# A decoder kernel's routing: logits and residual from the output projection, one scan for the places, one-hots on three engines

## Chip, core and metric

The kernel runs as one program on one core of a Trainium2 chip. The metric is the device time of one execution in microseconds (us). All operands are float32 unless said otherwise; the program is written by hand, with its own semaphores on each engine: PE (TensorE), DVE (VectorE), ACT (ScalarE), POOL (GpSimd) and SP (SyncE, which issues transfers).

## What is computed

Two decoder blocks on x of shape 32 x 64 x 128 (2048 tokens of 128 features), each sublayer followed by `x = layernorm(x + f(x))`. Block 0: a windowed self attention with its MLP, a causal windowed cross attention on a context, and a mixture of experts. Block 1: a linear attention, a recurrence, and a small attention on the seven best rows of each sequence. The change is about the end of the cross attention and the routing of the experts:

```python
# cross attention, last lines; then the norm
out = attn_out @ Wo.T + bo
x = _layernorm(x + out)
# experts: E = 8, K = 2, cap = 512
logits = xt @ wg
scores = softmax(logits)
gates_k, idx_k = top_k(scores, K)
gates_k = gates_k / sum(gates_k)
m = one_hot(idx_k, E) in the order (choice, token)
loc = sum((cumsum(m, axis=0) - 1) * m, axis=-1)
valid = loc < cap
disp = disp.at[idx_k, clip(loc)].add(xt * valid)
h = relu(disp @ w1 + b1); out = h @ w2 + b2
y = sum over the K choices of gates_k * valid * out[idx_k, loc]
```

## The kernel before, in words

The 2048 tokens are 16 tiles of 128 rows, worked in four quads of four tiles. Each engine runs its list in order; what another engine must wait for is a semaphore. A `Chain` object (`link`) makes an engine wait for its own last result.

**Self attention and its MLP.** `att_pe`, `att_dve`, `att_act` and `att_spread` (POOL, L383) work tile by tile. `norm1` on DVE and POOL norms the tiles behind it: POOL adds, takes the reciprocal root of the variance (`rstd_of`, L566 and L567), and makes three adds or products of a quad for the later residual (L682, L683, L685); DVE forms the shift (L1459) and then two columns of a bias (L1472). PE then loops over quads (L850 on): hidden layer (`hidden_self`, L814), the transposes of the next quad (L589), the keys and values of the cross attention (`keys_values`, L834 and L846), and the MLP's output (L863, bank 4). It works the keys of a quad only after DVE has taken the values before (`values_out`, L1513). DVE takes the MLP's output with L1488, norms it (`sum_quad`, L1491), adds the residual (`second_norm`, L1499) and norms again (`third_norm`).

**Cross attention.** The same helpers, with `add_bo` on POOL: after tiles 8 to 11 it forms `x_side = x + bo` for a quad (L709). DVE's step for a tile holds, among others, L493 (maximum), L509 and L511 (two steps on 16 elements) and L520. In the last two turns PE transposes the attention's output (`turn_out`, L925), ACT copies it (L1304), and PE multiplies by Wo (`project_out`, L931, one bank per quad). DVE adds `x_side` (L1536) and takes the statistics (L1479, L1482), POOL the root; DVE forms the shift of quads 0 and 1 and ACT norms them (L1310), DVE norms quads 2 and 3 (L544). SP stores each quad to `token_rows` (L634).

**Routing.** PE transposes the normed tiles (`ln_pe`, L589), ACT copies them (L595), PE multiplies by wg (`logits`, L915). DVE copies the logits (L1565), chooses twice (L1569 to L1576, eleven steps up to the second one-hot), and forms the gates around an exp of ACT (L1322). PE multiplies the one-hots by a matrix of ones and by one of earlier rows (L961, L962); DVE copies, scans (L1589) and combines these to the place of each choice (L1588 to L1613). It then builds two bf16 one-hots in four chunks, by slot (L1618) and by row (L1620), which PE multiplies in 32 products (L967); from that DVE computes which token row each place of an expert takes (L1628 to L1634, `place`). POOL gathers these rows with indirect transfers (`fetch`, L716) for four experts ahead, and scatters results (L730). Meanwhile ACT waits for DVE's L1638 with an Ln (L1329), forms `decay` and copies `wcomb` (L1333, L1335), after which PE runs ten filling matmuls (`keep`, L576) and the experts (`turn_in` L981, `hidden` L988, `output` L995).

## Time and profile before

| | |
|---|---|
| median of 3 runs | 444.09 us (440.9 to 446.13) |
| the profiled execution's own time | 440.14 us |
| its span in the profile | 438.3 us |
| PE busy | 365.4 us, 83% |
| DVE, ACT, POOL busy | 257.0, 194.5, 188.2 us |

The trace gives each instruction a start and a length in us from the span's start. An engine's idle time is shown with the one whose semaphore ended it. The chain of waits is followed back from the last instruction to whatever released each step. The granted clock is that of PE: 1.00 is 2.4 GHz, 0.50 is 1.2 GHz.

### The profile page before, as it was taken

To read this page: it belongs to the slowest core of one execution; us is meant where nothing else is said; L and a number is where in the kernel's file an instruction comes from. 1 tells how busy PE (TensorE), PEld (TensorE's weight loads), DVE (VectorE), ACT (ScalarE), POOL (GpSimd) and SP (SyncE) were. 2 spreads that over 40 slices of the span, in tenths; PEclk is the share of its full clock that TensorE was granted. 3 is DMA by queue.
4 is the path that set the end of the run, shared out by engine and by line. 5 is a ranking of instruction groups with operands and counts; after the bars stand their busy time and mean duration, and the time that the engine had idled before them with its cause. 6 is when DMAs were issued, how large, how long until landed. Compare 5 with 4: busy or idle time off the path is not lost.

```text
span 438.3 us, 8261 instructions
## 1 busy us (share of the span) xinstructions
PE 365.4 (83%) x3249; PEld 260.5 (59%) x3249; DVE 257.0 (59%) x742; ACT 194.5 (44%) x333; POOL 188.2 (43%) x232
## 2 busy tenths in 40 slices
PE   6999988999989999881489978797857988888780
PEld 2677775677767777761238756752635656765550
DVE  0788992689999899759600100022785788437430
ACT  1567775734577777521244433022362432124420
POOL 2234546853343520310376777772333437440002
PEclk9999999999999999995599999899889887859996
DMA  7999600000000000030011111117000000010000
GB/s 275 408 406 396 209 4 1 2 1 1 1 1 2 1 2 1 10 89 0 18 55 42 55 50 52 50 54 198 9 0 1 0 2 0 25 72 1 1 1 12
DMA packets 18358, 27.54 MB, mean 63 GB/s; under 512 B 2416, under 2 KB 13680, under 8 KB 17680
## 3 DMA queue, kind: packets, MB, share of 16 engines
q1 hardware_dynamic: 16208, 22.69, 14.5%
q0 software_dynamic: 2112, 4.33, 3.4%
q8 instruction: 26, 0.43, 0.4%
q14 instruction: 12, 0.10, 0.1%
HBM read 20.59 MB, written 6.42 MB: 62 GB/s over the span
## 4 chain that ended last, share of the span: by engine, by line
PE 57%; POOL 11%; DVE 11%; ACT 9%; issue 6%; DMA 4%; POOLq 0%; SPq 0%; DVEq 0%; ACTq 0%
PE bank L410 7%; PE bank L433 7%; PE bank L420 7%; PE bank L576 6%; POOL choice_rows L730 4%; POOL q_diag L716 4%; PE bank L589 3%; PE bank L995 3%; PE bank L863 3%; PE bank L988 2%; PE bank L814 2%; PE bank L393 2%; ACT x_tok L1310 2%; DMA q_diag<-in_q_self 1%; PE bank L872 1%
## 5 line engine op out<-in xcount | busy, mean ns | idle before, releaser
L576 PE MATMUL bank<-mask_bf,ident_bf 128*128 128x512 bf16 x206 | 59.5, 425 | 4.5 <-DVE mask_bf L1442 3.4
L493 DVE TENSOR_REDUCE neg_max<-bank 128x16 f32<-128x1024 f32 x34 | 41.5, 1222 | 19.4 <-PE bank L410 19.3
L383 POOL TENSOR_TENSOR scratch<-k_comp,con 128x512 f32<-128x512 f32 x32 | 33.4, 1047 | 37.6 <-PE bank L410 33.8
L465 ACT COPY probsT<-bank 128x1024 f32<-128x1024 f32 x34 | 34.4, 1012 | 26.3 <-PE bank L420 26.2
L716 POOL DMA_INDIRECT q_diag<-token_rows,place x32 | 30.8, 963 | 35.4 <-DVE place L1634 26.0
L476 ACT ACTIVATE probs<-probs 128x1024 f32<-128x1024 f32 x34 | 35.9, 1056 | 19.6 <-DVE probs L520 19.6
L433 PEld LDWEIGHTS bank<-v_pair,probsT 128*64 128x64 f32 x1088 | 34.7, 138 | 16.4 <-issue 10.8
L433 PE MATMUL bank<-v_pair,probsT 128*64 128x18 f32 x1088 | 37.9, 212 | 5.5 <-ACT probsT L465 4.6
L1665 DVE TENSOR_TENSOR probsT<-bank,mb 128x512 f32<-128x512 f32 x7 | 4.8, 691 | 62.2 <-PE bank L995 62.2
L410 PE MATMUL bank<-scratch,q_diag 64*128 64x256 f32 x272 | 39.5, 410 | 0.7 <-DVE scratch L383 0.5
L566 POOL TENSOR_SCALAR var_e<-mv 128x4 f32<-128x4 f32 x28 | 6.9, 247 | 75.8 <-DVE mv L1686 41.0
L420 PE MATMUL bank<-con,probs 128*128 128x128 f32 x272 | 36.9, 279 | 1.1 <-ACT probs L476 1.0
L576 PEld LDWEIGHTS bank<-mask_bf,ident_bf 128*128 128x128 bf16 x206 | 21.1, 109 | 27.2 <-issue 7.9
L730 POOL DMA_INDIRECT choice_rows<-probsT,place x32 | 31.2, 975 | 11.6 <-issue 8.8
L995 PEld LDWEIGHTS bank<-mw,hT 128*128 128x128 f32 x256 | 31.1, 197 | 4.5 <-issue 4.5
L995 PE MATMUL bank<-mw,hT 128*128 128x128 f32 x256 | 31.6, 280 | 0.9 <-ACT hT L1348 0.9
L410 PEld LDWEIGHTS bank<-scratch,q_diag 64*128 64x128 f32 x272 | 24.1, 190 | 13.9 <-issue 11.0
L420 PEld LDWEIGHTS bank<-con,probs 128*128 128x128 f32 x272 | 29.4, 141 | 3.2 <-ACT probs L476 1.8
L567 POOL TENSOR_TENSOR rstd<-var_e,neg_half 128x4 f32<-128x4 f32 x28 | 29.7, 1062 | 2.3
L988 PE MATMUL bank<-probs,mw 128*128 128x512 f32 x64 | 29.2, 599 | 1.5 <-ACT probs L1341 1.5
L1348 ACT ACTIVATE hT<-bank,mb 128x512 f32<-128x512 f32 x32 | 22.0, 687 | 18.2 <-PE bank L988 17.5
L589 PE MATMUL bank<-con,x_tok 128*128 128x128 f32 x80 | 19.1, 328 | 11.2 <-ACT x_tok L1310 7.1
(281 smaller groups left out, 678.8 us busy)
## 6 DMA issues: line engine op xcount, KB each, us to landing
mw<-in_mw SPq DMA_DIRECT2D x2, 2048.0 KB, 14.0
v_pair<-in_v_self SPq DMA_DIRECT2D x4, 576.0 KB, 11.2
q_diag<-in_q_self SPq DMA_DIRECT2D x4, 512.0 KB, 10.4
choice_rows<-hT SPq DMA_DIRECT2D x1, 2048.0 KB, 13.3
con<-in_const SPq DMA_DIRECT2D x1, 1249.5 KB, 15.1
k_comp<-in_k_self SPq DMA_DIRECT2D x4, 256.0 KB, 9.3
x_tok<-in_x SPq DMA_DIRECT2D x1, 1024.0 KB, 10.8
ctxT<-in_ctxT SPq DMA_DIRECT2D x1, 1024.0 KB, 9.6
```

The source lines that it names most:

```text
L383: mult(k_heads[:, i % 2], k_comp[:, i, :, None, :].to_broadcast([P, 2, HG, S]), hm, ALU.mult).then_inc(s["spread"], 1)
L410: last = nc.tensor.matmul(bank[:, 2 * (i % 2) + rg, g * 256:(g + 1) * 256], q_diag[r, i, g], k_heads[r, i % 2, g].rearrange("p h k -> p (h ...
L420: last = nc.tensor.transpose(bank[:, 4 + hp // 4, (hp % 4) * P:(hp % 4 + 1) * P], probs[:, i % 2, hp * P:(hp + 1) * P], ident)
L433: last = nc.tensor.matmul(bank[b * S:(b + 1) * S, 6 + i % 2, hp * VW:(hp + 1) * VW], probsT[:, i % 2, at:at + S], v_pair[:, 2 * i + b, hp] ...
L465: nc.scalar.copy(probsT[:, i % 2], bank[:, 4:6, :].rearrange("p a n -> p (a n)")).then_inc(s["evacuated"], 1)
L476: nc.scalar.activation(probs[:, i % 2], probs[:, i % 2], ACT.Exp).then_inc(s["exp"], 1)
L493: have_m = link.mark(nc.vector.tensor_reduce(m, sc, AX, ALU.max, negate=True))
L576: nc.tensor.matmul(bank[:, bk, :], ident_bf[:, :], mask_bf[:, 0, None, :].to_broadcast([P, 8, S]), start=True, stop=True)
L716: nc.gpsimd.indirect_dma_start(out=expert_x(e)[:, j], out_offset=None, in_=token_rows[:, :], in_offset=bass.IndirectOffsetOnAxis(ap=place[ ...
L730: nc.gpsimd.indirect_dma_start(out=choice_rows[:, :], out_offset=bass.IndirectOffsetOnAxis(ap=place[:, 1, at:at + 1], axis=0), in_=expert_ ...
L988: mm(bank[:, f], mw1[:, e, f * P:(f + 1) * P], probs[:, e % 2, 0:512], start=True, stop=True).then_inc(s_mh, 1)
L995: last = mm(cols4(out_bank(j), j), hT[:, v % 2, f, j * P:(j + 1) * P], mw2[:, v, f], start=f == 0, stop=f == FC - 1)
```

## The change

**Folding.** Products with wg are made ahead. Behind the self attention PE forms the column mean of wg and transposes Wo and bo; DVE makes `with_x = [ident | wg - mean]` and copies the transposes; PE, after the first `keys_values`, waits for these copies, forms Wo wg and bo wg, waits for DVE's copies of these, and goes on with L863. `with_o = [Wo | Wo wg]`.

**Projection.** For each tile PE adds the residual's product `xT x with_x` and `attention x with_o` in one PSUM group of 136 columns; the last eight are the logits before the norm's scaling. DVE adds a bias to these (`logits`), and bo to the first 128. The transposes, copies and products for the logits go, and POOL's `add_bo` too. For quad 3 ACT copies the projection, POOL adds bo and DVE takes the statistics after the choices. ACT norms all four quads, and the gates' difference is multiplied by rstd.

**Places.** The one-hots are bf16 (`chosen_bf`). Two products add up to the steps between one tile's place and the next, and DVE scans them straight from PSUM. Row and tile come from a division by rounding.

**One-hots.** The row one-hots are shared: chunks 0 and 1 on DVE, chunk 2 on ACT (eight Square and a Relu), chunk 3 as a subtraction on POOL and a comparison with zero on DVE. `token_rows` gets a zero row in front, so that a gather's place takes three steps. `place` comes first, and the gates after it. PE's filling matmuls change from 12 ahead of the choices to 16, and 16 more follow the rank products.

The diff's core:

```diff
             att_pe(pe, att["self"], NT, ident_bf[:, :], mb(0), True,
...
+            mm(bank[:, 4, 0:E], con_at("ones"), wg[:, :], start=True, stop=True)
+            tr(bank[:, 4, P:2 * P], wo[:, :], ident)
+            tr(bank[:, 4, 2 * P:3 * P], rows[:, 6], ident).then_inc(s_r["fold"], 1)
             pe.wait_ge(att["self"]["taken"], NT)
...
                 keys_values(q)
+                if q == 0:
+                    pe.wait_ge(s_r["folded"], 1)
+                    mm(bank[:, 4, 3 * P:3 * P + E], wo_turned, with_x[:, P:], start=True, stop=True)
+                    mm(bank[:, 4, 3 * P + E:3 * P + 2 * E], bo_turned, with_x[:, P:], start=True, stop=True).then_inc(s_r["fold"], 1)
                 if q == NQ - 1:
                     ln_pe(pe, ln["ln3"], 1, x_tok)
                 pe.wait_ge(s_hT, FC * q + FC)
                 if q >= 1:
                     pe.wait_ge(ln["ln2"]["stats"], 4 * q)
+                else:
+                    pe.wait_ge(s_r["folded"], 2)
...
             def project_out(q):
                 pe.wait_ge(s_oTs, q + 1)
                 for j in range(4):
-                    last = mm(cols4(2 + q, j), masked(q)[:, j * P:(j + 1) * P], wo[:, :], start=True, stop=True)
+                    if j % 2:
+                        residual(q, j)
+                    last = mm(projection(q)[:, j // 2, j % 2], masked(q)[:, j * P:(j + 1) * P], with_o, start=False, stop=True)
                 last.then_inc(s_wo, 1)
+
+            def residual(q, j):
+                t = 4 * q + j
+                mm(projection(q)[:, j // 2, j % 2], xT[:, t * P:(t + 1) * P], with_x, start=True, stop=False)
...
-            keep(2, 12)
+
+            keep(6, 16)
             pe.wait_ge(s_r["chosen"], 1)
-            oh = route("onehot", 2 * NT * E)
-            mm(bank[:, 1, E:256], con_at("ones"), oh[:, 0:256 - E], start=True, stop=True).then_inc(s_r["ranks"], 1)
-            mm(bank[:, 0, 0:256], con_at("earlier_row"), oh, start=True, stop=True).then_inc(s_r["ranks"], 1)
+            steps = bank[:, 0, 0:256].rearrange("p (e n) -> p e n", e=E)
+            oh = chosen_bf[:, :, :].rearrange("p n e -> p e n")
+            mm(steps, earlier_bf, oh, start=True, stop=False)
+            mm(steps[:, :, 1:], later_bf, oh[:, :, 0:TOPK * NT - 1], start=False, stop=True).then_inc(s_r["ranks"], 1)
+            keep(2, 16)
...
             norm_act("ln4", 1)
-            for q in range(NQ):
-                ln_act(act, ln["ln4"], q)
+            act.wait_ge(s_r["logits"], NQ)
+            cp(tiles22(work[:, NT - 4:NT]), projection(NQ - 1)[:, :, :, 0:P]).then_inc(s_oTs, 1)
+            norm_act("ln4", 2)
+
+            act.wait_ge(s_r["rows"], 1)
+            for n in range(16, 24):
+                off = link.mark(A(rank_hot[:, n], row_index_bf[:, :], ACT.Square, bias=route("row_of", TOPK * NT)[:, n:n + 1], scale=-1.0))
+            link.wait(off)
+            A(rank_hot[:, 16:24], rank_hot[:, 16:24], ACT.Relu, bias=con_at("ones")[:, 0:1], scale=-1.0).then_inc(s_r["exp"], 1)
+
+            norm_act("ln4", 3)
...
                 ts(cols[:, at:at + 2], cols[:, 0:2], con_at("own_half")[:, b:b + 1], HD ** -0.5, ALU.mult, ALU.mult)

+            dve.wait_ge(s_r["fold"], 1)
+            stt(with_x[:, P:], bank[:, 4, 0:E], -1.0 / P, wg[:, :], ALU.mult, ALU.add)
+            cp(wo_turned, bank[:, 4, P:2 * P])
+            cp(bo_turned, bank[:, 4, 2 * P:3 * P]).then_inc(s_r["folded"], 1)
+            cp(with_x[:, 0:P], ident)
+            cp(with_o[:, 0:P], wo[:, :])
...
                 values_out(q)
+                if q == 0:
+                    dve.wait_ge(s_r["fold"], 2)
+                    cp(with_o[:, P:], bank[:, 4, 3 * P:3 * P + E])
+                    cp(logit_bias, bank[:, 4, 3 * P + E:3 * P + 2 * E]).then_inc(s_r["folded"], 1)
...
+            cp(row_index_bf[:, :], con_at("row_index"))
+            cp(earlier_bf, con_at("earlier_row"))
+            ts(later_bf, con_at("earlier_row"), -1.0, 1.0, ALU.mult, ALU.add)
...
+            shift(ln["ln4"], 2)
+            dve.wait_ge(s_wo, NQ)
+            logits(NQ - 1).then_inc(s_r["logits"], 1)
+            dve.wait_ge(s_r["logits"], NQ)
...
+            dve.wait_ge(s_side, NQ + 1)
+            told_quad(ln["ln4"], NQ - 1, [link.n] * 4)
...
+            link(nc.vector.tensor_tensor_scan(run, con_at("scan_carry"), bank[:, 0, 0:256], 0.0, ALU.mult, ALU.add))
+            v_at = at.rearrange("p (n e) -> p n e", e=E)
+            link(tt(v_at, run.rearrange("p (e n) -> p n e", e=E), chosen_bf[:, :, :], ALU.mult))
+            link(nc.vector.tensor_reduce(rank, v_at, AX, ALU.add))
+            link(ts(tile_of, rank, 0.5 - P / 2, 1.0 / P, ALU.add, ALU.mult))
+            link(ts(tile_of, tile_of, ROUND, ROUND, ALU.add, ALU.subtract))
+            stt(row_of, tile_of, float(-P), rank, ALU.mult, ALU.add).then_inc(s_r["rows"], 1)
...
+            pool.wait_ge(s_r["rows"], 1)
+            tt(rank_hot[:, 24:32], row_index_bf[:, None, :].to_broadcast([P, 8, P]),
+               route("row_of", TOPK * NT)[:, 24:32, None].to_broadcast([P, 8, P]), ALU.subtract).then_inc(s_r["rows"], 1)
```

DVE's list after `rows` is then: `held`, the two parts of `told_bf`, the shift of quad 3, the four chunks, three steps to `place[:, 0]` (which release the gathers), two to `place[:, 1]`, the gates' difference times rstd, and after ACT's exp the gates and their validity.

## Rows read from the trace of the kernel before

**Rows 1.** The page's part 4: shares of the chain that ended last, by engine.
```profile
PE 57%; POOL 11%; DVE 11%; ACT 9%; issue 6%; DMA 4%; POOLq 0%; SPq 0%; DVEq 0%; ACTq 0%
```

**Rows 2.** Chain of waits, 70 to 96 us: start, us, what.
```profile
75.85 3.77 PE bank L863 x32
79.62 3.45 PE bank L814 x8
...
94.35 1.07 PE bank L834 x16
```

**Rows 3.** Timeline, 74 to 98 us: start, us, engine, line, operation [idle before <-releaser].
```profile
80.28 1.23 DVE L1459 SCALAR_TENSOR_TENSOR var_e<-mv,rstd 128x4 f32<-128x4 f32 x1 [3.95 <-POOL rstd L567]
...
82.77 1.38 DVE L1513 TENSOR_TENSOR v_pair<-bank,rows 64x512 f32<-64x512 f32 x2
82.79 1.27 POOL L685 TENSOR_TENSOR x_tok<-x_tok,rows 128x512 f32<-128x512 f32 x1
...
84.19 0.89 DVE L1488 TENSOR_TENSOR work<-bank,routing 128x128 f32<-128x128 f32 x4
```

**Rows 4.** Busy time in stretches: us, PE, PEld, DVE, ACT, POOL, granted PE clock, DMA.
```profile
199.00:199.50 0.50, 0.00 (x0) 0.00 (x0) 0.47 (x2) 0.14 (x1) 0.00 (x0) 0.58 0.00 0
...
219.50:220.00 0.50, 0.50 (x4) 0.25 (x3) 0.00 (x0) 0.00 (x0) 0.50 (x1) 0.94 0.45 123
```

**Rows 5.** Timeline, 134 to 159 us, beside the bias add.
```profile
151.57 1.28 POOL L709 TENSOR_TENSOR x_side<-x_tok,rows 128x512 f32<-128x512 f32 x1
...
151.79 1.08 DVE L509 TENSOR_SCALAR neg_max<-neg_max 128x16 f32<-128x16 f32 x1
...
154.61 1.11 PE L433 MATMUL bank<-v_pair,probsT 128*64 128x18 f32 x32 [0.80 <-DVE work L524]
```

**Rows 6.** Timeline, 174 to 222 us, the projection and norm.
```profile
176.62 1.06 PE L931 MATMUL bank<-wo,scratch 128*128 128x128 f32 x8
...
183.31 3.19 ACT L1310 ACTIVATE x_tok<-work,var_e,rstd 128x128 f32<-128x128 f32 x8
...
184.67 1.04 POOL L567 TENSOR_TENSOR rstd<-var_e,neg_half 128x4 f32<-128x4 f32 x1
```

**Rows 7.** The same timeline, choices, one-hots and places.
```profile
193.47 0.29 DVE L1569 TENSOR_REDUCE routing<-routing 128x16 f32<-128x128 f32 x1
...
196.70 0.29 DVE L1573 TENSOR_TENSOR routing<-routing 128x128 f32<-128x128 f32 x1
...
203.78 0.69 DVE L1618 TENSOR_TENSOR probs<-room_bf,told_bf 128x512 bf16<-128x512 bf16 x1
204.39 1.22 DVE L1620 TENSOR_TENSOR scratch<-row_index_bf,rank_row 128x1024 bf16<-128x1024 bf16 x1
...
211.59 0.19 DVE L1628 TENSOR_SCALAR routing<-bank 128x32 f32<-128x32 f32 x1 [0.22 <-PE bank L967]
```

**Rows 8.** Timeline, 210 to 224 us, the start of the experts.
```profile
213.40 0.20 ACT L1329 ACTIVATE cols<-cols 128x1 f32<-128x1 f32 x1 [14.25 <-DVE cols L1638]
...
214.01 1.22 POOL L716 DMA_INDIRECT q_diag<-token_rows,place  x1 [25.96 <-DVE place L1634]
...
216.91 3.63 PE L576 MATMUL bank<-mask_bf,ident_bf 128*128 128x512 bf16 x10 [0.36 <-ACT wcomb L1335]
...
220.67 0.66 PE L981 MATMUL bank<-con,q_diag 128*128 128x128 f32 x4
```

**Rows 9.** Groups by form: busy us, mean ns, idle before.
```profile
L671 POOL TENSOR_TENSOR work<-work,x_tok 128x128 f32<-128x128 f32 x16 | 7.3, 456 | 30.0 <-DVE work L524 30.0
...
L476 ACT ACTIVATE probs<-probs 128x1024 f32<-128x1024 f32 x34 | 35.9, 1056 | 19.6 <-DVE probs L520 19.6
```

**Rows 10.** Groups of DVE, 170 to 214 us.
```profile
L1479 DVE BATCH_NORM_STATS2 stats<-work 128x6 f32<-128x128 f32 x16 | 3.5, 281 | 0.1
...
L1589 DVE TENSOR_TENSOR_SCAN routing<-con,routing 128x256 f32<-128x256 f32 x1 | 0.7, 691 | 0.0
...
L1596 DVE TENSOR_TENSOR routing<-routing 128x256 f32<-128x256 f32 x1 | 0.4, 426 | 0.0
```

More of the change, by code:

```diff
@@ L347, in build @@
         s_oT, s_oTs, s_wo = sem("s_oT"), sem("s_oTs"), sem("s_wo")
-        s_r = names("route", "logits", "chosen", "ranks", "gap", "exp", "slots", "rows", "hot", "found")
+        s_r = names("route", "logits", "chosen", "ranks", "gap", "exp", "slots", "rows", "hot", "found", "fold", "folded")
         s_moe = names("experts", "zeroed", "stored", "turned", "xT", "out")
@@ L911, in cross_queries @@
                     pe.wait_ge(s_v_free, NQ)
-            def logits(q):
-                pe.wait_ge(ln["ln4"]["yT_out"], ln["ln4"]["quads"] + q + 1)
-                for t in range(4 * q, 4 * q + 4):
-                    last = mm(bank[:, 0, t * E:(t + 1) * E], xT[:, t * P:(t + 1) * P], wg[:, :], start=True, stop=True)
-                return last
             def turn_out(q):
@@ L1531, in last_norms, with logits @@
                     third_norm(NQ - 1)
+            bo4 = rows[:, 6:7].to_broadcast([P, 4, D])
+            def logits(q):
+                lq = route("logits", NT * E).rearrange("p (t e) -> p t e", e=E)[:, 4 * q:4 * q + 4]
+                return tt(tiles22(lq), projection(q)[:, :, :, P:], tiles22(logit_bias[:, None, :].to_broadcast([P, 4, E])), ALU.add)
             def projected(q):
@@ L1534, in projected @@
                 dve.wait_ge(s_wo, q + 1)
-                dve.wait_ge(s_side, NQ + q + 1)
-                n = link.mark(tt(work[:, r], bank[:, 2 + q].rearrange("p (t n) -> p t n", n=P), x_side[:, r], ALU.add))
+                n = link.mark(tt(tiles22(work[:, r]), projection(q)[:, :, :, 0:P], tiles22(bo4), ALU.add))
+                logits(q).then_inc(s_r["logits"], 1)
                 told_quad(ln["ln4"], q, [n] * 4)
@@ L1578, in _ @@
                     last.then_inc(s_r["chosen"], 1)
-            tt(route("e", NT), route("m1", NT), route("m0", NT), ALU.subtract).then_inc(s_r["gap"], 1)
-            dve.wait_ge(s_r["exp"], 1)
+            dve.wait_ge(s_side, NQ + 1)
+            told_quad(ln["ln4"], NQ - 1, [link.n] * 4)
+            n = TOPK * NT
+            run, at = route("run", 256), route("at", 256)
+            rank, row_of, tile_of = route("rank", n), route("row_of", n), route("tile_of", n)
+            dve.wait_ge(s_r["ranks"], 1)
@@ new lines, in _ @@
+            a, late, own = route("tot", E * CT), route("run", E * CT), route("at", E * CT)
+            dve.wait_ge(s_r["found"], 1)
+            link(nc.vector.tensor_reduce(a, bank[:, 4, 0:E * 2 * CT].rearrange("p (s c) -> p s c", c=2), AX, ALU.add))
+            link(ts(late, a, float(T + 1), float(-T), ALU.is_ge, ALU.mult))
+            tt(place[:, 0], late, a, ALU.add).then_inc(s_r["slots"], 1)
+            link(stt(own, a, 1.0, con_at("spare"), ALU.is_lt, ALU.mult))
+            stt(place[:, 1], a, -1.0, own, ALU.add, ALU.add)
@@ L1582, in _ @@
+            link(tt(route("e", NT), route("m1", NT), route("m0", NT), ALU.subtract))
+            tt(route("e", NT), route("e", NT), rstd[:, :], ALU.mult).then_inc(s_r["gap"], 1)
+            dve.wait_ge(s_r["exp"], 2)
             link(ts(route("m0", NT), route("e", NT), 1.0, None, ALU.add))
@@ L1631, in _ @@
-            link(stt(own, a, 0.0, con_at("spare"), ALU.is_lt, ALU.mult))
-            link(tt(late, late, a, ALU.add))
-            link(ts(place[:, 0], late, 0.0, None, ALU.max))
-            tt(place[:, 1], own, a, ALU.add).then_inc(s_r["slots"], 1)
+            valid = route("logits", n)
+            link(ts(valid, rank, float(CAP), None, ALU.is_lt))
+            tt(route("m0", n), route("m0", n), valid, ALU.mult).then_inc(s_r["slots"], 1)
             dve.wait_ge(s_lin["consts"], 1)
```

172 lines of the change are left out of this document (78 added, 94 removed).

## The prediction

> **What bounds the kernel now.** I read the page first: its chain is 57% TensorE, with DVE, POOL and ACT at 9 to 11% each [rows 1]; no engine is the bound over the span, so every stage is read from its own last wait. The diff touches three: the first block's MLP, the cross attention, and the routing up to the experts. The chain of waits from 70 to 96 us comes next. There it runs on PE without a gap from the first quad's MLP output (L863, 75.85) into the second quad's hidden layer (L814, 79.62), and reaches the third quad's keys at 94.35 by way of ACT, POOL and DVE [rows 2]. The timeline beside it shows where DVE is meanwhile: it waits 3.95 us for POOL's last rstd, runs L1459 at 80.28, and starts quad 0's values at 82.77 [rows 3]. In the routing, the timeline shows DVE as the chain: the maximum starts at 193.47, the second choice ends at 196.99, the one-hots start at 203.78, the places start at 211.59, and the first gather at 214.01 [rows 7, 8]. The experts behind it start when the PE has turned the first gathered quad, at 220.67 [rows 8]; from there to the first expert's result PE is not interrupted.
>
> **Part 1, the folding, on the path.** PE gets three small products ahead of a wait for DVE, which are hidden by that wait, and after the first keys and values it waits for `folded` 1, ahead of L863 of quad 0, and for `folded` 2 right before it. Both are raised by DVE, and its new copies stand in program order behind norm1's last shift and L1472, so behind 82.77 [rows 3]. Nothing in that DVE queue waits for PE, so it does not come earlier or later. Step by step: multiply-add and two copies from PSUM at some 0.2 us each, from 82.77 to 83.4. PE, idle since 75.85, forms Wo Wg and the bias in four passes, some 0.6 us (a 128-row pass takes 0.13 of the 1.06 us that eight take [rows 6]): 84.05. DVE meanwhile copies ident and Wo. POOL's L685 holds 82.79 to 84.06 [rows 3], and I count these two behind it: 84.35. `values_out(0)` takes 1.38 [rows 3], to 85.7, and two copies of eight columns bring `folded` 2 at 85.95. L863 so starts 10.1 us later. PE has been empty for 10 us but for four passes. Its granted clock was down to half 1.5 us after the rank products ended at 198, and came back 2.6 us into the filling matmuls of 216.91 [rows 4, 8]; some 3 us of L863 at half rate cost 1.5. Sum: **+11.6 us**. Behind L863 stand, in this order and on the chain, hidden layer 1, ACT, three POOL adds, DVE's second norm and values 1 [rows 2], all moved as they are. The 4.6 us for which quad 0's result lay ready before DVE took it at 84.19 [rows 3] do not help, as the chain leaves PE through L814 and not through that result. Bounds: 9.65 if the copies pass POOL and the clock stays up (82.77 plus 0.6, 0.4, 1.36 and 0.35 is 85.5); 13 if the copies and the values are each held once more by POOL (1.3 us).
>
> **Part 2, the bias add out of POOL.** Four adds L709 go. While they run, DVE's sixteen-element L509 takes 1.08 us, and where PE waits next for DVE (154.61, 0.80 idle) [rows 5] that delay reaches the path; for the three others PE was busy throughout. **-0.85 us**, bounds 0 and -1.
>
> **Part 3, the projection.** Each tile takes two products of 136 columns in place of one of 128. Eight passes take 1.06 [rows 6]; sixteen of 136 columns 2.0. Quad 0 delays the last weighing from 177.89 to 178.65. From there: weighing to 179.7, quad 1 to 181.7, transposes and ACT's copy to 182.95 with quad 2's first residuals under the copy, quad 2's other twelve passes to 184.5, transposes and copy to 185.7, quad 3 to 187.35.  The sixteen transposes, four copies and sixteen logits products that followed are gone, and logits come with each quad. The last are not read at 187.35, as DVE first does shift 2, which waits for POOL's rstd of quad 2. Statistics of quad 2 end at 186.5, rstd takes 0.25 and 1.04 [rows 6] with its hand-overs: 188.1. Logits at 188.4, the maximum at 188.45 against 193.47.
>
> **Part 4, the choices.** The eleven steps of 0.32 are the same, 193.47 to 196.99 [rows 7]. But ACT, behind eight activations (3.19 us [rows 6]), copies quad 3's projection at 188.8 to 189.4, and POOL adds the bias for 1.28 us [rows 5] just then; DVE's two-input steps wait about 1.0. Chosen at 192.95: **4.05 us** won at this point.
>
> **Part 5, places and one-hots.** After `chosen`: statistics of quad 3 (four of 0.21, as they overlap, four of 0.09: 1.2), which hide PE's rank products; a scan of 256 0.7, a product and a sum of 256 0.44 each [rows 10]; three small steps 0.6; `held` 0.3; two told steps 0.4; a shift 0.13: 4.2. To this I add POOL's share. Its subtraction has 1024 elements; POOL's add takes 0.456 us for 128 and 1.28 for 512 [rows 5, 9], so 2.35 by the slope. It starts at 196.65, when DVE has the told steps ahead, and DVE waits until about 199. First one-hot at 199.45, 6.5 after `chosen`; before 6.8. So the shorter arithmetic is nearly given back: **0.3 won**. The one-hots: four slot products of 0.6, two rank comparisons of 1.14 [rows 7] and one single-input comparison of 0.35 make 5.05 where they were 7.0; with the last eight products the places begin at 205.3: **2.0 won**. ACT's share, eight squares at 0.39 [rows 6] and a relu of 1.06 [rows 9], is done at 200.7, and PE first asks at 203.5: cover 2.8 us. If Square needed a table it would still fit. The last token rows are normed at 202.3 and stored some 3 us later, just ahead. The gather's places take three steps and not seven: **0.9 won**. Sum 7.25; first gather at 206.8.
>
> **Part 6, what is late next.** The gates' exp used to come before the places; ACT's Ln, the decay and the copies of `wcomb` follow it in ACT's order, and PE's ten filling matmuls follow these. Before, Ln ran at 213.40, the filling began at 216.91 and took 3.63, and the turn at 220.67 had been waiting for the gather just as long [rows 8]. Now DVE does two place steps, the gap (two), and after ACT's exp five gate steps, some 2.2 us, before `one_plus`: Ln at 209.1, filling 212.65 to 216.3. The first gathered quad is there at 206.8 plus 6.6, 213.4. So PE turns at 216.35, and 2.9 of the 7.25 are lost: **-4.3 us** at the experts, which run on from there as before. Bounds: -3 (POOL's subtraction 3 us, or ACT's rows late) and -7.5 (neither POOL operation holds DVE, 3.2 more).
>
> A rule bears on parts 4 and 5. The trace shows L509 at 1.08 us beside L709, 0.17 in other tiles [rows 5]. The Trainium skill, "SBUF", section "Who interferes with whom", says that a DVE instruction with two SBUF inputs or in a two-port mode and a GpSimd instruction that reads SBUF lock each other out for the whole instruction. By it the sharing of the one-hots gives the middle case here; without it, the sum would be 3.2 us lower.
>
> **Sum**: 11.6 - 0.85 - 4.3 = **+6.4 us** on the profiled execution's own 440.14 us (span 438.3 and 1.8 around it): 446.6. That execution is at the low end of 440.9 to 446.13 and its neighbours; on the median of 444.09 the same sum gives **450.5 us**. About 1%, 4.4 us, is what a measurement of this kernel can tell from no change.
>
> **Rivals.**
> *A, forecast, 0.60:* as above, 450.5; own range 447 to 454.
> *B, no port conflict in the routing, 0.17:* all of part 5's DVE steps run free of POOL, and the copies at 83 too. Then 11.15 (9.65 and 1.5 for the clock) less 0.85 and 7.5: +2.8, 446.9, within 1%. For it: most of DVE's work in the cross attention reads PSUM and runs beside POOL's multiply unhurt; against it: L509's row, and L1459, a four-column step that takes 1.23 us beside POOL's adds [rows 3].
> *C, routing returns next to nothing, 0.13:* the 136-column groups, POOL's 1024 elements or the later `wcomb` cost 3 us more, 453.5.
> *D, not slower, 0.10:* the fold's wait does not hold L863, since DVE reaches its copies before PE asks. It decides at 75.85: each us that the copies come later holds PE one more, and the sign turns when L863 and its slow clock together cost 5.15 us, so near 81.0. Then the change is -5.1, 439.0. For it: the statistics of DVE end by 76.2, and only one shift is left; against it: that shift waited 3.95 us for POOL and started at 80.28 [rows 3], and POOL's adds before it depend on nothing that the change moves.
>
> So slower by over 1%: A almost whole, C: 0.69; within 1%: B and an edge of A: 0.22; faster by over 1%: D: 0.09. The range 444.5 to 455.5 takes in B, A and C and leaves out D.
>
> **What would show it.** PE idle for 7.6 us from about 75.9, then a few passes, then L863 near 86 at half granted clock; the keys of quad 2 at about 106. If L863 stands at 76, D holds and the forecast is wrong. L509 at 0.17 in all tiles. Between last projection and first maximum about 1 us, with a shift in it. One DVE step of the choices stretched by about 1 us beside POOL's add, and a hole of about 2 us ahead of the one-hots beside POOL's subtraction; without them, B. The filling matmuls ending 2 to 3 us after the first four gathers have landed; if PE waits for the gather, part 6 is wrong and another 2.9 us are won.

## The result, and the profile after

The changed kernel takes 446.48 us (median of four runs, 445.65 to 449.66). The kernel before, on the same chip and with the runs shown earlier among its four, takes 442.5 us. The ratio is 1.0136, 95% interval 1.0078 to 1.0193. That is +6.0 us of 442.5, between 3.5 and 8.5. The ratios here and below compare fast runs alone (some executions of the kernel before, on other chips, ran slower, up to 463.77 us, most of them at a lower granted clock), so they are not the quotient of the medians. Forecast were +6.4 us, and 450.5 us on a base of 444.09. The two medians are 4.0 us apart, which lies within the interval too. Of the 4.0 us between forecast and measured time 1.6 are the base.

The profiled execution took 445.65 us (span 443.8, mean granted clock 0.919). Its first MLP matmuls (L814 before, L835 after) start 1.07 us earlier than those of before, 66.64 against 67.71, in a stage that the change does not touch. Distances are therefore read from a common instruction.

The page's shares of the chain hardly moved against [rows 1]; they do not tell what happened:

```profile
PE 58%; POOL 12%; DVE 11%; ACT 9%; issue 6%; DMA 3%; POOLq 0%; SPq 0%; DVEq 0%; ACTq 0%
```

**The fold.** Timeline of PE, 64 to 130 us: start us, busy us, engine, line, operation, and in brackets the idle time before and what ended it [rows 2]:

```profile
66.64 3.67 PE L835 MATMUL bank<-xT,aw 128*128 128x512 f32 x8 [1.02 <-ACT xT L1277]
...
73.63 1.15 PE L870 MATMUL bank<-wv,ctxT 128*64 128x64 f32 x32
82.25 0.60 PE L882 MATMUL bank<-inside,told_bf 128*128 128x8 f32 x2 [7.47 <-DVE chosen_bf L1519]
82.70 0.58 PE L883 MATMUL bank<-inside,chosen_bf 128*128 128x8 f32 x2
84.87 5.54 PE L893 MATMUL bank<-aw,hT 128*128 128x128 f32 x32 [1.59 <-DVE inside L1573]
90.24 3.60 PE L835 MATMUL bank<-xT,aw 128*128 128x512 f32 x8
```

PE stands still for 7.47 us where it had run on. L893 (L863 before) starts 18.23 us behind the first MLP matmuls (8.07 in the same timeline of before), and the next quad's hidden layer 23.60 (11.74). That is 10.16 us of waiting and 1.70 of slow matmuls. Timeline of DVE in that wait [rows 3]:

```profile
79.17 1.22 DVE L1501 SCALAR_TENSOR_TENSOR var_e<-mv,rstd 128x4 f32<-128x4 f32 x1 [3.92 <-POOL rstd L582]
...
81.92 0.28 DVE L1519 COPY chosen_bf<-bank 128x128 f32<-128x128 f32 x1
82.12 0.90 DVE L1520 COPY inside<-con 128x128 f32<-128x128 f32 x1
...
84.57 0.16 DVE L1573 COPY inside<-bank 128x8 f32<-128x8 f32 x1
```

The copy that releases PE (L1519) stands behind the shift L1501, which waits 3.92 us for POOL. The copies that PE does not need stand ahead of L1573. Stretches (us, busy PE, PEld, DVE, ACT, POOL, granted clock, DMA share, GB/s) show the clock [rows 4]:

```profile
80.00:84.00 4.00, 1.02 (x4) 0.93 (x4) 3.99 (x10) 0.00 (x0) 2.85 (x3) 0.50 0.00 0
85.00:88.00 3.00, 3.00 (x15) 3.00 (x16) 0.00 (x0) 0.00 (x0) 0.00 (x0) 0.50 0.00 0
```

**The routing.** Timeline, 184 to 216 us [rows 5 to 8]:

```profile
184.51 1.11 PE L448 MATMUL bank<-v_pair,probsT 128*64 128x18 f32 x32 [0.29 <-ACT probsT L480]
...
198.27 0.29 DVE L1626 TENSOR_REDUCE routing<-routing 128x16 f32<-128x128 f32 x1
199.05 1.29 POOL L727 TENSOR_TENSOR work<-work,rows 128x512 f32<-128x512 f32 x1 [1.11 <-ACT work L1352]
199.57 0.93 DVE L1630 TENSOR_TENSOR chosen_bf<-routing 128x128 bf16<-128x128 f32 x1
...
206.09 1.90 POOL L731 TENSOR_TENSOR scratch<-row_index_bf,routing 128x1024 bf16<-128x1024 bf16 x1 [1.16 <-DVE routing L1649]
206.25 1.83 DVE L1654 TENSOR_SCALAR told_bf<-inside,con 128x128 bf16<-128x128 f32 x1
...
208.40 0.69 DVE L1659 TENSOR_TENSOR probs<-chosen_bf,told_bf 128x512 bf16<-128x512 bf16 x1
...
215.77 1.22 POOL L736 DMA_INDIRECT q_diag<-token_rows,place  x1 [7.78 <-DVE place L1673]
```

From the weighing at 184.51 (174.65 before) the first maximum comes after 13.76 us (18.82), the second choice ends after 17.93 (22.34), the first one-hot starts after 23.89 (29.13), and the first gather after 31.26 (39.36). Of the DVE steps that start while one of POOL's two operations runs, L1630 (0.93 us) and L1654 (1.83) are the stretched ones; the reduction L1629, which starts within POOL's add at 199.25, keeps its 0.29 us. L731 started 0.16 us before the DVE step that it held.

**The experts.** The same timeline, 215 to 242 us [rows 8]. The first turn is PE's transposing of the first gathered tokens (L1014, L981 before):

```profile
217.57 0.20 ACT L1371 ACTIVATE cols<-cols 128x1 f32<-128x1 f32 x1
...
219.92 0.80 PE L1006 MATMUL bank<-wcomb 128*128 128x128 f32 x2 [5.50 <-ACT wcomb L1375]
221.08 4.26 PE L591 MATMUL bank<-mask_bf,ident_bf 128*128 128x512 bf16 x10 [0.36 <-ACT wcomb L1377]
225.18 0.60 PE L1014 MATMUL bank<-con,q_diag 128*128 128x128 f32 x4
...
239.22 0.69 DVE L1716 TENSOR_TENSOR probsT<-bank,mb 128x512 f32<-128x512 f32 x1 [16.57 <-PE bank L1028]
240.70 1.00 POOL L751 DMA_INDIRECT choice_rows<-probsT,place  x1 [4.86 <-DVE probsT L1716]
```

PE does not wait for the gather at 225.18 but for its own filling, and that for ACT. The turn comes 40.67 us behind the weighing at 184.51 (46.02 before): of the 8.10 us won at the first gather, 5.35 are left.

### The profile page after: what moved, and what is told of

The parts are those of the page before. It is cut to its first block, busy times and chain, and to the rows that moved or that the text cites. A ratio compares the mean times of both kernels' runs of the same rounds, so it can differ in the third digit from the quotient of the medians.

```text
span 443.8 us, 8265 instructions
## 1 busy us (share of the span) xinstructions
PE 369.0 (83%) x3250; PEld 263.9 (59%) x3250; DVE 247.7 (56%) x739; ACT 198.9 (45%) x347; POOL 186.6 (42%) x230
## 4 chain that ended last, share of the span: by engine, by line
PE 58%; POOL 12%; DVE 11%; ACT 9%; issue 6%; DMA 3%; POOLq 0%; SPq 0%; DVEq 0%; ACTq 0%
PE bank L448 7%; PE bank L425 7%; PE bank L435 7%; PE bank L591 6%; POOL choice_rows L751 4%; POOL q_diag L736 3%; PE bank L1028 3%; PE bank L893 3%; PE bank L604 3%; PE bank L1021 2%; PE bank L835 2%; PE bank L408 2%; POOL rstd L582 1%; DMA q_diag<-in_q_self 1%; PE bank L902 1%
## 5 line engine op out<-in xcount | busy, mean ns | idle before, releaser
L591 PE MATMUL bank<-mask_bf,ident_bf 128*128 128x512 bf16 x219 | 62.0, 423 | 4.5 <-DVE mask_bf L1484 3.4
L591 PEld LDWEIGHTS bank<-mask_bf,ident_bf 128*128 128x128 bf16 x219 | 22.5, 107 | 29.8 <-issue 9.0
L425 PE MATMUL bank<-scratch,q_diag 64*128 64x256 f32 x272 | 38.6, 402 | 0.7 <-DVE scratch L398 0.5
L1028 PEld LDWEIGHTS bank<-mw,hT 128*128 128x128 f32 x256 | 32.2, 203 | 4.5 <-issue 4.5
L1028 PE MATMUL bank<-mw,hT 128*128 128x128 f32 x256 | 32.8, 286 | 0.9 <-ACT hT L1390 0.9
L604 PE MATMUL bank<-con,x_tok 128*128 128x128 f32 x64 | 15.7, 338 | 11.0 <-ACT x_tok L1343 7.1
```

Source lines behind the costliest of these rows:

```text
L425: last = nc.tensor.matmul(bank[:, 2 * (i % 2) + rg, g * 256:(g + 1) * 256], q_diag[r, i, g], k_heads[r, i % 2, g].rearrange("p h k -> p (h ...
L591: nc.tensor.matmul(bank[:, bk, :], ident_bf[:, :], mask_bf[:, 0, None, :].to_broadcast([P, 8, S]), start=True, stop=True)
L1028: last = mm(cols4(out_bank(j), j), hT[:, v % 2, f, j * P:(j + 1) * P], mw2[:, v, f], start=f == 0, stop=f == FC - 1)
```

## The experiments

Theory: PE's wait for the fold, set by where DVE's instructions stand, costs 11.9 us. The routing wins 8 us at the first gather and loses about a third of it to ACT's chain. GpSimd's two operations stretch one DVE step each. Rivals: the stall is absorbed further on and the routing itself is slow; or something else takes the stall's place. The twelve runs (ten kernels, and the changed kernel and the kernel before once more) were made on four chips. The chip of the first measurement is called the first chip. Times are compared with the kernel before on the same chip, and stages through the traces. Marks used: first MLP matmuls (M), first maximum (X), first gather (G). "As forecast" below refers to the expectation printed there.

**The fold alone, on the kernel before.** Edit: the products, copies and waits of the changed kernel; nobody reads what they give.

```diff
+            tr(bank[:, 4, 2 * P:3 * P], rows[:, 6], ident).then_inc(s_r["fold"], 1)
...
+                if q == 0:
+                    pe.wait_ge(s_r["folded"], 1)
+                    mm(bank[:, 4, 3 * P:3 * P + E], wo_turned, with_x[:, P:], start=True, stop=True)
...
+            cp(bo_turned, bank[:, 4, 2 * P:3 * P]).then_inc(s_r["folded"], 1)
```

> The kernel before with the fold of the changed kernel added at its places on TensorE and DVE (column sums, two turned matrices, two products, seven DVE instructions, all the waits) and its results used by nobody; routing and projection are those of the kernel before. Theory: the fold alone costs 11.6 us, the kernel takes 442.5 + 11.6 = 454 us, 1.026 of the kernel before; the second MLP matmuls of quad 0 start 10.1 us later. Rival one (later slack absorbs the stall): 1.000 to 1.010. Rival two (the changed kernel's 136-column passes or its routing are the loss): 1.000.

Measured: 470.23 us, ratio 1.032 (1.018 to 1.046), that is +14.6 us with an interval of 8 to 21. The timeline of PE is sharper, with M at 66.56:

```profile
82.18 0.60 PE L867 MATMUL bank<-inside,told_bf 128*128 128x8 f32 x2 [7.47 <-DVE room_bf L1492]
...
84.80 5.75 PE L878 MATMUL bank<-aw,hT 128*128 128x128 f32 x32 [1.59 <-DVE inside L1546]
90.38 3.60 PE L820 MATMUL bank<-xT,aw 128*128 128x512 f32 x8
```

The wait is the same to 0.01 us. The second hidden layer comes 23.82 us behind M against 11.74, and G 158.3 us behind M against 146.5 in the kernel before on another chip (below): 11.8 us, with the old routing. Nothing between absorbs it. Both rivals fall. (The time of +14.6 us is above the 12.1 us that the trace shows, within its interval.)

**DVE's fold instructions moved forward.**

```diff
+                if i == 20:
+                    dve.wait_ge(s_r["fold"], 1)
+                    stt(with_x[:, P:], bank[:, 4, 0:E], -1.0 / P, wg[:, :], ALU.mult, ALU.add)
+                    cp(wo_turned, bank[:, 4, P:2 * P])
+                    cp(bo_turned, bank[:, 4, 2 * P:3 * P]).then_inc(s_r["folded"], 1)
+                if i == 22:
+                    cp(with_x[:, 0:P], ident)
...
                 if i % 4 == 0 and 0 <= q < NQ:
```

> The changed kernel with DVE's fold instructions moved forward in its program and nothing else: the three that release TensorE's fold products stand ahead of the first norm's third shift (DVE idles there for 0.94 us), the other four ahead of its last shift (3.92 us idle). Theory (TensorE loses 11.7 us because DVE's program order puts the fold behind the last shift, 10.1 us of waiting and 1.7 us of half clock): the second MLP matmuls of quad 0 start at about 76 us instead of 84.87 us and take 3.8 us instead of 5.54 us; of the 11.7 us some 1.0 to 1.3 us stay, because the products, two copies and the hand-overs still stand between keys and MLP; the kernel takes 435 to 437 us, 0.985 to 0.99 of the kernel before. Rival one (the fold isn't what holds TensorE, or something later in the MLP, the norms of quad 3 or the cross attention takes the stall's place): the cross attention starts less than 4 us earlier than the 125.41 us of the changed kernel and the time stays at 443 us or more. Rival two (the routing is what made the kernel slower and the stall is absorbed): no change against the changed kernel, 446 us.

Measured: 446.66 us, ratio 0.9852 (0.978 to 0.993). Timeline of PE and DVE, M at 66.40, and a stretch with the clock:

```profile
74.72 0.37 PE L883 MATMUL bank<-inside,chosen_bf 128*128 128x8 f32 x2
75.06 1.28 DVE L1504 COPY inside<-wo 128x128 f32<-128x128 f32 x1
76.64 5.44 PE L893 MATMUL bank<-aw,hT 128*128 128x128 f32 x32 [1.55 <-DVE inside L1507]
```

```profile
76.60:80.00 3.40, 3.37 (x16) 3.40 (x17) 1.05 (x1) 1.40 (x4) 3.23 (x4) 0.52 0.00 0
```

The 7.47 us of waiting are gone and the ratio falls as forecast, but a part of the theory fails: 1.55 us of idle time still halved the clock, and L893 took 5.44 us, not 3.8. From M to the next hidden layer it is 15.51 us, 3.77 more than before, where 1.0 to 1.3 were expected. The idle time itself comes from a copy that PE does not need: L1504 of Wo (0.21 us in the changed kernel, L1521) takes 1.28 us while POOL works, and stands ahead of the two copies that PE waits for. The cross attention's first scores come at 117.00, 8.3 us earlier than in the changed kernel, so the first rival falls too.

**The wait filled.** Edit: `keep(0, 33)`, matmuls of no use, ahead of PE's wait for `folded` 1 and `keep(0, 6)` behind the two products.

> The changed kernel with 33 matmuls of no use in TensorE's 7.47 us wait for the fold and 6 more behind the two products; the wait itself stays. It splits the stall into waiting and clock. Theory: the granted clock stays at full speed, the second MLP matmuls of quad 0 take 3.8 instead of 5.54 us while they start where they did (84.9 us), and the kernel takes 446.5 - 1.7 = 444.8 us, 1.005 of the kernel before. Rival (the half clock isn't from the idle time, or DVE is bound there anyway and the faster matmuls wait): no gain, 446.5 us; if the filling runs past the fold, a loss of up to 1 us.

Measured: 456.24 us, ratio 1.0033 (0.9993 to 1.0072), on the same chip. Timeline of PE, M at 68.67:

```profile
76.74 7.30 PE L591 MATMUL bank<-mask_bf,ident_bf 128*128 128x512 bf16 x33
...
86.96 3.81 PE L896 MATMUL bank<-aw,hT 128*128 128x128 f32 x32 [0.70 <-DVE inside L1576]
90.60 3.60 PE L835 MATMUL bank<-xT,aw 128*128 128x512 f32 x8
```

L896 starts 18.29 us behind M, as in the changed kernel (18.23), and takes 3.81 us; the next hidden layer is at 21.93 against 23.60. So the clock is 1.7 us of the loss and the waiting is the rest. The ratio agrees with the 1.005 expected, but the changed kernel was not run on this chip, so the time alone does not show the 1.7 us.

**The fold in time on both sides.** PE's products between the keys and the values of quad 0, DVE's two last copies right behind the third shift:

```diff
                 project(wk, ctxT, 5, q)
+                if q == 0:
+                    pe.wait_ge(s_r["folded"], 1)
...
+                if i == 21:
+                    dve.wait_ge(s_r["fold"], 2)
+                    cp(with_o[:, P:], bank[:, 4, 3 * P:3 * P + E])
+                    cp(logit_bias, bank[:, 4, 3 * P + E:3 * P + 2 * E]).then_inc(s_r["folded"], 1)
```

> The changed kernel with the fold where both sides have it in time: TensorE's two products between the keys and the values of quad 0, DVE's three instructions that release them ahead of the norm's third shift, its two copies of the products right after that shift, the two copies that nobody waits for last. Theory: nothing is left of the wait (10.1 us) nor of the half clock behind it (1.7 us; the first try left 1.55 us of idle time and the MLP matmuls still took 5.44 us), the second MLP matmuls of quad 0 start at about 75.5 us and take 3.8 us; left are the two products, 0.8 us. Against the changed kernel beside it -11 us, 0.975 of it; against the kernel before about 0.988. Rival (the half clock comes from something else than the idle time): the matmuls still take 5.4 us, -9.3 us.

with the changed kernel once more beside it:

> The changed kernel once more, unaltered, as the base for the three kernels run beside it on the same chip. On the chip of the first four experiments the expert stage was slower than in the profiles of before and after (second expert result 11.4 us after the first instead of 7.4 us), in kernels of both routings. Expected 1.0136 of the kernel before, as first measured; if this chip has the slow expert stage too, the difference of the first result's time may shrink to 1.005, because the expert stage then waits for its gathers and takes up a part of what precedes it.

Measured: the changed kernel 456.13 us, 1.0066 (1.0031 to 1.0101) of the kernel before; with the fold in time 446.53 us, 0.9853 (0.9801 to 0.9905). Timeline of PE:

```profile
78.60 1.15 PE L874 MATMUL bank<-wv,ctxT 128*64 128x64 f32 x32
79.89 3.81 PE L893 MATMUL bank<-aw,hT 128*128 128x128 f32 x32
```

No wait and full clock. The same placement in the next kernel, whose first matmuls ran at full clock, has the next hidden layer 12.47 us behind M, where the changed kernel of this chip has 23.83: 11.4 us less in the traces, 9.6 in the medians of the fold in time (446.53 against 456.13; 11 forecast). The rival for the clock falls.

**ACT's chain ahead of the routing result.** Edit: the four exps moved behind `turned_out`, DVE's two small steps ahead of shift 2, Ln, negation and decay behind `norm_act("ln4", 2)`.

```diff
             norm_act("ln4", 2)
+            act.wait_ge(s_lin["one_plus"], 1)
+            link(A(col("log_gamma"), col("t2"), ACT.Ln))
+            link(nc.scalar.mul(col("log_gamma"), col("log_gamma"), -1.0))
+            A(decay[:, :], con_at("decay_steps"), ACT.Exp, scale=col("log_gamma")).then_inc(s_lin["consts"], 1)
```

> The changed kernel with ACT's and DVE's chain for the linear layer's constants (four exps, two small DVE instructions, Ln, a negation, the decay matrix, with its two table loads) moved ahead of the routing result, into idle time of ACT at 192.7 to 194.8 us and at 200.5 to 206.05 us. Theory (the expert stage starts 2.75 us later than the gathers allow because TensorE's combined weight waits for this chain behind the exp): the filling matmuls ahead of the first expert start at about 216.5 us instead of 221.08, the first expert's tokens are turned as soon as they have landed, about 222.4 us instead of 225.18 us, and the kernel takes 446.5 - 2.8 = 443.7 us, 1.003 of the kernel before. Rival one (the landing of the gathers, not the chain, decides): the turn stays at 225 us, no gain. Rival two (the chain collides with the squares that ACT builds for the routing, or with the last shift on DVE): the first gather is later than 215.8 us by up to 1 us and the gain is 1.8 us or less.

Measured: 457.38 us, ratio 1.0091 (1.0047 to 1.0135). Timeline of PE, G at 215.68:

```profile
217.00 4.45 PE L591 MATMUL bank<-mask_bf,ident_bf 128*128 128x512 bf16 x10 [0.36 <-ACT wcomb L1377]
222.57 0.66 PE L1014 MATMUL bank<-con,q_diag 128*128 128x128 f32 x4 [1.11 <-DMA q_diag<-token_rows,place]
223.90 3.70 PE L1021 MATMUL bank<-probs,mw 128*128 128x512 f32 x8 [0.67 <-issue]
...
239.37 5.29 PE L1021 MATMUL bank<-probs,mw 128*128 128x512 f32 x8 [2.81 <-ACT probs L1383]
```

The first turn is 6.89 us behind G, not 9.41, and now waits for the gather: part 6 of the prediction is shown, and what the chain costs at this place is 2.5 us. Its second rival is seen in small: from X to G it is 17.82 us against 17.50, so the moved chain costs 0.3 us there. The time does not follow; at the third expert PE idles 2.81 us. From G to the end of the last expert result this run took 99.0 us, the filled kernel on the same chip 95.1. What took those 4 us more is not settled; the profiled execution (459.46 us) was itself 2.1 us above the median of its kernel.

**Both together, on the chip of the fold in time.**

> The kernel with the fold in time and, on top, the early chain for the linear layer's constants of e4_lin_early. Theory: 2.6 us less than the kernel with the fold in time alone, as the turn of the first expert's tokens showed in that run (222.57 us instead of 225.18 us with the first gather at the same time), because the first expert result releases GpSimd's scatters and those pace the experts. Rival (the experts are paced by the landing of later gathers, as the first four runs suggest, where the gain at the first turn was gone at the second expert): no difference, within 0.5 us.

Measured: 444.17 us, ratio 0.9815 (0.9756 to 0.9874). The median is 2.4 us below that of the fold in time alone, but the intervals overlap for the most part, and the trace supports only a fifth of it: the first expert result comes 23.22 us behind G against 23.66. PE ran out of filling 1.08 us before the tokens landed:

```profile
211.21 0.66 PE L1014 MATMUL bank<-con,q_diag 128*128 128x128 f32 x4 [1.08 <-DMA q_diag<-token_rows,place]
212.54 5.40 PE L1021 MATMUL bank<-probs,mw 128*128 128x512 f32 x8 [0.68 <-issue]
```

**GpSimd's one-hots back to DVE.** Edit: L731 is dropped, DVE's comparison for `c != 2` in place of `c < 2`.

> The changed kernel with the fourth chunk of row one-hots built by DVE like the first two instead of a subtraction on GpSimd and a compare with zero on DVE. It measures the port conflict of the routing. Theory (the subtraction of 1.90 us holds DVE's told step, 1.83 us instead of 0.29 us): the told step takes 0.3 us again, the first one-hot starts 1.5 us earlier, the fourth chunk takes DVE 1.1 to 1.2 us instead of 0.42 us, the first gather is 0.8 us earlier: -0.8 us. Rival (the told step is slow of itself, bf16 with a stride of two): the told step stays at 1.8 us and the kernel loses 0.7 us.

Timeline of DVE:

```profile
206.37 0.30 DVE L1650 TENSOR_SCALAR told_bf<-inside,con 128x128 bf16<-128x128 f32 x1
...
211.66 1.22 DVE L1658 TENSOR_TENSOR scratch<-row_index_bf,routing 128x1024 bf16<-128x1024 bf16 x1
```

The step that builds `told_bf` (L1654 in the changed kernel) takes 0.30 us, the rival falls, and from X to G it is 16.76 us against 17.50: -0.74 us, as forecast. The time, 456.68 us or 1.0079 (1.0044 to 1.0114), shows no gain over 1.0066: the 0.74 us are too few for this measurement.

**The last residual on DVE.** Edit: ACT's copy L1352 and GpSimd's add L727 dropped, DVE adds bias and projection behind the second choice. Timed once.

> The changed kernel with the residual of the last quad added on DVE behind the second choice, in place of ACT's copy and GpSimd's bias add of 1.29 us beside DVE's choice. It measures the port conflict of step 4. Theory (the first choice took 0.92 us instead of 0.29 us because the bias add holds the port): it takes 0.29 us, the second choice ends 0.6 us earlier (3.5 instead of 4.17 us behind the start of the first maximum); the add costs DVE 0.69 us in front of the statistics and the scan starts 0.5 us later than now, measured from the second choice; first gather within 0.2 us of the changed kernel, measured from the first maximum (17.5 us). Rival (the first choice is slow because it writes bf16): 0.92 us stays, the first gather is 0.6 us later.

```profile
200.60 0.29 DVE L1625 TENSOR_TENSOR chosen_bf<-routing 128x128 bf16<-128x128 f32 x1
```

With X at 199.31 the second choice ends 3.53 us behind it (4.17), the scan starts at 204.54, and G is 17.38 us behind X (17.50). All as forecast: the hold of the choice by GpSimd's add is worth 0.64 us, and undoing it by this way wins nothing. The time was 457.08 us.

**The four bias adds put back.** Timed once; the sums are used by nobody.

> The changed kernel with GpSimd's four bias adds of 1.27 us of the kernel before put back at their places in the cross attention, their results used by nobody. It measures step 2 alone. From the first scores of the cross attention to the weighing ahead of the first projection TensorE took 60.04 us before and 59.17 us in the changed kernel. Theory (the adds stood between key spreads on GpSimd and cost 0.85 us): 60.0 us. Rival (the 0.87 us come from the new residual matmuls and their order): 59.2 us.

```profile
185.47 1.11 PE L448 MATMUL bank<-v_pair,probsT 128*64 128x18 f32 x32 [0.30 <-ACT probsT L480]
```

The first scores of the cross attention are at 125.37, so the stretch is 60.10 us. Part 2 is shown. The time was 446.04 us, and that of the kernel before on the same chip 446.14, one run each: where the traces have the changed kernel 6 us behind, these two show nothing. Runs of one kernel on one chip spread by 4 us and more, so neither number is evidence for or against it.

**Everything together, and the kernel before once more.** The best kernel joins the fold in time, the early chain, one-hots without GpSimd, and `keep(5, 13)` for `keep(5, 10)`.

> The kernel with the fold in time, the early chain for the linear layer's constants and no one-hots on GpSimd, with 13 instead of 10 filling matmuls ahead of the first expert: in the run with the early chain TensorE ended its filling 1.08 us before the gathered tokens landed, and the first expert's eight matmuls then took 5.40 us instead of 3.70 us. Theory: no idle time ahead of the first turn, 3.70 us for these matmuls, first expert result 21.6 us behind the first gather instead of 23.2 us (with) and 23.7 us (without the early chain); the first gather 0.7 us earlier by the one-hots. Time 442 us on a chip on which the kernel before takes 454 us, 0.973 of it. Rival (the pace of the later gathers takes up what the first expert gains, as the four tries of the first chip suggest): the time stays at that of the fold in time and the early chain, 0.9815.

> The kernel before, unaltered, for its profile on a chip whose expert stage is like that of the experiments. In the profile of the changed kernel on the second chip the stage from the first expert result to the last takes 70.9 us against 58.8 us in its first profile. Expected here: if the chip sets this, 70 to 71 us too (58.1 us in the first profile of before), and everything ahead of the first gather as in that profile, 146.3 us from the first MLP matmuls to the first gather. If it is the changed kernel's own loss, 58 us.

Measured: all together 443.89 us, ratio 0.9840 (0.9777 to 0.9903); the kernel before 451.9 us in its one run. Timeline of PE in the kernel with all, G at 204.28:

```profile
205.62 5.03 PE L591 MATMUL bank<-mask_bf,ident_bf 128*128 128x512 bf16 x13 [0.36 <-ACT wcomb L1373]
211.10 0.66 PE L1010 MATMUL bank<-con,q_diag 128*128 128x128 f32 x4 [0.45 <-DMA q_diag<-token_rows,place]
212.43 3.70 PE L1017 MATMUL bank<-probs,mw 128*128 128x512 f32 x8 [0.67 <-issue]
...
227.73 3.70 PE L1017 MATMUL bank<-probs,mw 128*128 128x512 f32 x8 [2.49 <-ACT probs L1379]
```

0.45 us of idle time are left ahead of the turn, where none was expected. The first expert's matmuls take 3.70 us, at full clock, as expected, and still the first expert result is 22.98 us behind G and not 21.6: here the rival holds. The four kernels with the fold early or in time, 0.9815 to 0.9853 of the kernel before, can't be told apart. All four are faster than the kernel before by 1.5 to 1.9%, with intervals clear of 1, and the two that ran beside the changed kernel took 9.6 and 12.0 us less than it.

The traces of before and changed kernel on two of these chips (one each), DVE's last expert result and POOL's first gather. The kernel before:

```profile
212.19 1.22 POOL L716 DMA_INDIRECT q_diag<-token_rows,place  x1 [26.18 <-DVE place L1634]
...
304.89 0.49 DVE L1663 TENSOR_TENSOR probsT<-bank,mb 128x128 f32<-128x128 f32 x2 [3.24 <-remote]
```

The changed kernel:

```profile
217.16 1.22 POOL L736 DMA_INDIRECT q_diag<-token_rows,place  x1 [7.78 <-DVE place L1673]
...
311.65 0.29 DVE L1714 TENSOR_TENSOR probsT<-bank,mb 128x128 f32<-128x128 f32 x1 [1.19 <-remote]
```

From G to the end of the last result: 93.2 us before, 94.8 us changed. On the first chip it was 79.1 and 82.5. The stage is 12 to 14 us longer on these chips in either kernel, and the changed one loses 1.6 us in it where it lost 3.4. Ahead of it the chips agree: M to G is 146.54 us in the kernel before, and was 146.30. So of the 3 us by which the change cost less on the later chip (1.0066 of 454.13 is +3.0, against +6.0) this stage would explain 1.8. Both steps are weak: the two kernels' traces are of two chips, and the intervals of +3.0 (1.4 to 4.6) and +6.0 (3.5 to 8.5) overlap, so the difference itself may be chance.

## Why the prediction was right

Measured in the two profiled executions, with the terms of the prediction:

- **Part 1, the fold: right, 0.3 us too small.** L893 10.16 us late (10.1 predicted), slow clock 1.70 (1.5), sum 11.86 (11.6). The fold alone on the old kernel gives 12.1 at the same place, the fill shows the clock's part, and the placement takes away all but 0.7. The order inside came true too: PE released by L1519, the ident copy held by POOL's add (0.90 us).
- **Part 2: right.** 60.04 to 59.17 us, -0.87 (-0.85); with the adds back 60.10. L509 (L524 in the changed kernel) takes 0.17 us in all tiles, as said.
- **Part 3: right.** 5.06 us won at the first maximum (5.02). As forecast, DVE first waited for POOL's rstd of quad 2 to do its shift.
- **Part 4: right in kind, 0.4 us off.** 4.41 us won at the choice (4.05). The term that was mis-sized is the hold of DVE's choice by POOL's add: 1.0 put, 0.64 measured, and confirmed by taking the add away.
- **Part 5: right in kind, mis-sized.** First one-hot 5.24 us won (4.35). POOL's subtraction was put at 2.35 us by the slope of f32 adds; in bf16 it took 1.90. The other two terms came out as put: one-hots 2.01 us won (2.0), the gather's places 0.85 (0.9). First gather 8.10 won (7.25).
- **Part 6: right, 0.2 us off.** Of what was won at the gather 2.75 us were lost at the turn (2.9); PE's filling ended after the landing, as said, and moving ACT's chain brought the turn forward by 2.5. Inside this term two errors cancelled: Ln came 1.80 us behind the first gather and not 2.35, and the ten filling matmuls took 4.26 us and not 3.63, as the granted clock stayed at 0.50 until about 225 us, some 4 us into the filling, where the prediction had it back after 2.6 us as in the kernel before. Not forecast was a smaller loss behind it, 0.5 us at POOL's first scatter (below).

At POOL's first scatter the changed kernel is 6.02 us behind, counted from M: 11.86 less 0.87, less 5.35, plus 0.5 for the hand-over, and 0.1 less from the stretches between. Forecast were 6.4. That this is met so closely is in part luck, as errors cancelled: 1.05 us more were left at the turn (5.35 against 4.3), 0.26 more lost in the fold and 0.5 in the hand-over. Over the whole span it is 6.57.

Rival D, the fold in time, is excluded by the products' start at 82.25 us. Built as an experiment it gave -6.7 us by the ratio 0.9853, with an interval of -4.3 to -9.0 that takes in its price of -5.1 us. In the trace of the next kernel (same placement, and ACT's chain early) M to G is 138.35 us against 146.54, so 8.2 us are won at the gather, and the experts take 0.7 back (93.9 us to the last result against 93.2). Rival B, no port conflict, is excluded by the two held steps, together 2.2 us. Rival C, a routing that returns next to nothing, is excluded by the 8.10 us at the gather and the 5.35 left at the turn.

The Trainium skill, "SBUF — State Buffer", section "Who interferes with whom", says that issue order decides which of the two engines is blocked. Here L731 started at 206.09 and the DVE step at 206.25 took 1.83 us, against 0.30 without L731: the trace agrees, for the one order that it shows. The prediction had used only that they exclude each other.

## What to carry over

A helper computation with small results is priced not by its instructions (two products, seven copies, about 2 us) but by where its hand-overs stand in each engine's program: here a place in DVE's queue behind an unrelated wait of 3.92 us, and what stood with it, cost 11.9 us, and moving the same instructions ahead of that wait gave back 11; 0.7 us for PE's products stay. When a result moves earlier, list what its consumer waits for besides it: ACT's constants, which nobody had needed early, cost a third of the routing's gain. A placement that leaves 1 to 2 us of idle TensorE can cost as much again in clock as a long wait; whether it does has to be read from the granted clock behind it (next section).

## What the runs showed of the hardware that was not expected

- **A short gap can cost the clock as much as a long one, but its length alone does not tell.** Behind 1.55 us of idle time the MLP matmuls took 5.44 us at a granted clock of 0.52, behind 7.47 and 1.59 us 5.54 us; with no gap 3.81. Gaps of 0.68 and 0.72 us at the same place in the kernel before left no mark (1.07 us for the sixteen passes behind, as everywhere). But longer gaps left none either. In the changed kernel PE idles 1.90 us ahead of the rank products, the granted clock stays at 1.00, and the sixteen filling matmuls behind take 3.64 us, as at full clock:

```profile
202.49 0.61 PE L991 MATMUL bank<-chosen_bf,told_bf 128*128 128x256 bf16 x1 [1.90 <-DVE chosen_bf L1630]
...
203.37 3.64 PE L591 MATMUL bank<-mask_bf,ident_bf 128*128 128x512 bf16 x16
```

  And ahead of the first expert's eight matmuls, gaps of 1.11 and 0.67 us left them at 3.70 us in the kernel with the early chain, while 1.08 and 0.68 us at the same place made them 5.40 in the next (both shown above). What decides between the two is open here.
- **The expert stage depends on the chip.** From first gather to last result 79.1 us on one chip and 93.2 on another for the same kernel, before; for kernels with the new routing 82.5 and 80.9 on two chips, 93.5 to 99.0 on the three others. On those three the second expert result follows the first after 10 to 13 us, on the other two 7.4. In the filled kernel, for instance, PE's transposes of the gathered tokens are recorded at once, yet ACT, which copies them, starts 1.8 and 8.3 us after their end (fourth and fifth expert), and PE's next eight matmuls take 6.53 us instead of 3.70, as after idle time. Late landing of gathers would look like this; it wasn't tried by itself and stays open.
- **A hand-over of 0.5 us more.** From the first expert result to POOL's scatter it took 0.97 us in the kernel before (POOL idle 1.72 and 3.88 us) and 1.48 us in the changed one (4.86, and 4.22 to 5.43 in the experiments). It goes with the longer idle time of POOL, but also with the kernel: the fold alone on the kernel before has 0.97 at 4.01 us of idle time. That the idle time is the cause is only argued.
